# A graph and mixture-of-experts kernel: quads to octets, and routed tiles inside the gather stage from per-expert bins in DRAM

## The reference, cut to what matters

```
x = x + gnn(layernorm(x))           # x: 12500 nodes x 256
x = x + ffn(layernorm(x))

gnn(f):  agg[d] = sum over edges (s -> d) of weight * f[s]    # 212,500 edges, sorted by d
         return agg @ W.T + b
ffn(f):  H = gelu(f @ W1 + b1)                 # 256 -> 1024
         probs = softmax(H @ Wg + bg)          # 8 experts
         e = argmax(probs)                     # per node
         return probs[e] * (H @ Wd[e] + bd[e])  # 1024 -> 256
```

## Time and profile before

| what | before |
|---|---|
| median of 3 runs | 3659.71 us (3659.63 to 3661.93) |
| profiled execution | 3686.61 us, span 3684.6 us |
| granted TensorE clock, mean | 0.706 of full speed |
| busy PE, POOL | 56%, 49% of the span |
| busy DVE, ACT | 31%, 12% |
| moved by DMA | 420.31 MB, mean 114 GB/s |

### The profile page before, as it was taken

How to read it: one execution, slowest core, us unless ns; L and a number is a source line. 1 busy time by engine, 2 the same in 40 slices (tenths; PEclk the granted TensorE clock), 3 DMA queues, 4 the chain that set the end, 5 groups by cost and what they waited for, 6 DMA issues and landing times.

```text
span 3684.6 us, 40719 instructions
## 1 busy us (share of the span) xinstructions
PE 2061.4 (56%) x10526; PEld 1319.5 (36%) x10527; DVE 1151.1 (31%) x3507; ACT 443.2 (12%) x847; POOL 1822.5 (49%) x1988
## 2 busy tenths in 40 slices
PE   0134555455535554455445544555355548599998
PEld 0112332233323332233223322332233324488887
DVE  8121332233323332233223322332133224733332
ACT  5000000000000000000000000000000002043343
POOL 1656445644565445544664455444644540055554
PEclk9995666566656666566656656666566658799999
DMA  8323332333333332333233323332333231455554
GB/s 358 88 82 98 97 103 84 115 99 98 104 91 106 100 101 83 113 100 101 84 115 100 102 81 111 98 102 86 105 103 100 82 92 63 154 180 180 181 184 139
DMA packets 153598, 420.31 MB, mean 114 GB/s; under 512 B 33320, under 2 KB 67499, under 8 KB 150880
## 3 DMA queue, kind: packets, MB, share of 16 engines
q0 software_dynamic: 100032, 300.27, 27.6%
q1 hardware_dynamic: 53536, 119.73, 8.8%
HBM read 328.02 MB, written 92.82 MB: 114 GB/s over the span
## 4 chain that ended last, share of the span: by engine, by line
PE 38%; another core or an unknown queue 33%; issue 15%; DVE 7%; DVEq 5%; ACT 1%; DMA 0%; POOL 0%; ACTq 0%; POOLq 0%
PE psH L557 8%; PE psE L507 6%; PE psA L638 3%; PE psG L638 2%; PE psH L638 2%; PE psE L638 2%; PE psA L578 2%; PE psG L499 2%; PE psR L499 2%; PE psA L535 2%; DVEq L301 2%; DVE rows L942 1%; DVEq L295 1%; PE psG L564 1%
## 5 line engine op out<-in xcount | busy, mean ns | idle before, releaser
L387 POOL DMA_INDIRECT big<-xn_table,src_i x1664 | 1590.8, 956 | 1427.4 <-PE psG L499 620.8
L507 PE MATMUL psE<-place,parts 128*128 128x64 f32 x1664 | 450.8, 433 | 1015.3 <-DVE parts L853 778.4
L507 PEld LDWEIGHTS psE<-place,parts 128*128 128x128 f32 x1664 | 382.6, 324 | 1280.6 <-DVE parts L853 871.7
L557 PE MATMUL psH<-xn2T,w 128*128 128x512 f32 x800 | 427.9, 692 | 128.6 <-issue 64.5
L450 ACT ACTIVATE hidT<-psH,b 128x512 f32<-128x512 f32 x200 | 136.4, 687 | 2447.2 <-remote 1006.6
L499 PE MATMUL psR<-big,sel_narrow 128*32 128x256 f32 x1664 | 216.8, 613 | 289.4 <-issue 289.4
L557 PEld LDWEIGHTS psH<-xn2T,w 128*128 128x128 f32 x800 | 173.4, 223 | 347.8 <-issue 267.6
L860 DVE TENSOR_TENSOR big<-psE,big 128x128 f32 x416 | 121.2, 291 | 545.1 <-remote 294.3
L853 DVE COPY parts<-psR 128x256 f32<-128x256 f32 x208 | 88.0, 423 | 518.6 <-remote 461.2
L499 PE MATMUL psG<-big,sel_narrow 128*32 128x256 f32 x1664 | 217.6, 613 | 0.0
L864 DVE TENSOR_TENSOR place<-iota,shift_f 128x256 f32<-128x256 f32 x104 | 44.4, 427 | 447.7 <-issue 447.7
(11 more groups left out here) (194 smaller groups left out, 2193.4 us busy)
## 6 DMA issues: line engine op xcount, KB each, us to landing
row_table<-rows SPq DMA_DIRECT2D x25, 2064.0 KB
big<-xn_table,src_i POOLq DMA_INDIRECT x1664
big<-in_x SPq DMA_DIRECT2D x10, 1280.0 KB, 17.5
xn_table<-big SPq DMA_DIRECT2D x10, 1280.0 KB, 12.9
big<-in_x SPq DMA_DIRECT2D x25, 512.0 KB
row_table<-big SPq DMA_DIRECT2D x25, 512.0 KB, 3.0
big<-in_Wd SPq DMA_DIRECT2D x8, 1024.0 KB, 12.0
hidT<-in_dstT SPq DMA_DIRECT2D x2, 840.0 KB, 30.3
```

The source lines that it names most:

```text
L387: nc.gpsimd.indirect_dma_start(out=xring[:, h * STEP_TILES + j, :], out_offset=None, in_=xn_dram[:, :], in_offset=bass.IndirectOffsetOnAxi ...
L507: mm = nc.tensor.matmul(psE[q % 2][:, k * NARROW:(k + 1) * NARROW], parts[:, q % 2, k * P:(k + 1) * P], place[:, q, :], start=True, stop=True)
L557: mm = nc.tensor.matmul(psH[c % 2][:, :], w1[:, k, c * P:(c + 1) * P], xn2T[:, k, :], start=(k == 0), stop=(k == KC - 1))
```

## The change

**Octets.** A gather step is now two octets of 8 tiles. All 16 partial matmuls run in a row and raise `s_edge_mm` once, by 16; DVE copies both octets at once (128x512), PE places both (8 matmuls for a window of 80 nodes each in place of 64) and signals once, DVE adds twice. The weights of the next step's one-hots come behind the additions.

**The group step** is split into part A and part B, and with `LATER = 0` a group's part B stands directly behind its part A. Part A is the GNN product, the residual and the normalisation, with two routed tiles on PE beside it. Part B is the transposes, `hidden` and the logits, two more routed tiles, then the sort of the group's own 512 nodes by expert: rank matmuls over one-hots, a permutation as a matrix (DVE), 16 matmuls of 128x260 that put the rows in order, ACT copies, a store to `sorted_dram`, and 15 DRAM-to-DRAM copies of blocks into one bin per expert (`bin_dram`), from places that a plan made by DVE names. Rows in the bins are 260 wide: residual or normalised values and the probability, not the 1024 hidden values, which are neither transposed nor stored any more.

**A routed tile** is 128 rows of one bin. It loads the rows, the 1 MB of its expert's weights and the bias on SP, in a ring of two; it computes hidden anew (16 matmuls of 128x128 and 8 gelus), then multiplies by the expert's weights (8 matmuls), and its result goes to `done_dram`. 4 tiles per group make 100 early tiles (the first groups' have nothing to work on but run), and 16 late tiles follow behind the last group. When all gathers are issued and read, POOL brings back the 100 early results and scatters them, 16 at a time from the three sections, then the late ones. The routing of all nodes at once, and the loading of all weights, are gone.

The accumulator's ring has 6 slots in place of 8, and the PSUM banks are laid out anew. Core of the diff:

```diff
-QUAD = 4
-QUADS = STEP_TILES // QUAD
-NARROW = 64
 SECTIONS = 3
+OCT = 8
+OCTS = STEP_TILES // OCT
+SPAN = 80
 LANES = 32
+HALF_LANES = 16
...
+STEPS = NG + ITEMS
+LATER = 0
...
+            def load_tile(r, row, expert):
+                i = r % RING2
+                if r >= RING2:
+                    sp.wait_ge(s_o2, r - RING2 + 1)
+                sp.dma_start(xr[:, i, :], bin_dram[bass.ds(row, P), :]).then_inc(s_xl[i], 16)
+                sp.dma_start(wd[:, i, :, :].rearrange("p c o -> p (c o)"),
+                             Wd[bass.ds(expert, 1), :, :].rearrange("a p f -> p (a f)")).then_inc(s_wl[i], 16)
...
+            def store_tile(r):
+                sp.wait_ge(s_o2, r + 1)
+                sp.dma_start(done_dram[r * P:(r + 1) * P, :], obuf[:, r % RING2, :]).then_inc(s_os[r % RING2], 16)
...
+                sp.wait_ge(s_plan, f + 2)
+                for a in range(0, BLOCKS, 5):
...
+                    for one, other in zip(froms, tos):
+                        sp.dma_start(bin_dram[bass.ds(other, BLOCK), :],
+                                     sorted_dram[bass.ds(one, BLOCK), :]).then_inc(s_cp, 16)
...
+            for f in range(NF):
+                r0, r1, r2, r3 = tiles_of(f)
+                plan = tile_plan(0, PER_GROUP)
+                sp.sem_inc(s_seen, 1)
+                load_tile(r0, *plan[0])
+                load_tile(r1, *plan[1])
+                store_tile(r0)
+                load_tile(r2, *plan[2])
+                if f < LAST:
+                    sp.wait_ge(s_xn2, f + 1)
+                    load_x(f + 1)
+                store_tile(r1)
+                load_tile(r3, *plan[3])
+                store_tile(r2)
+                store_tile(r3)
+                nq = QB if f < LAST else LAST_QB
+                sp.wait_ge(s_ev, f * QB + nq + 1)
+                sp.dma_start(sorted_dram[0:nq * P, :].rearrange("(q p) c -> p q c", p=P),
+                             sorted_rows[:, 0:nq, :]).then_inc(s_sst, 16)
+                sp.wait_ge(s_sst, 16 * (f + 1))
+                copy_blocks(f)
...
+            def scatter_batch(b):
+                h = b % SECTIONS
+                pool.wait_ge(s_back[h], 16 * (b // SECTIONS + 1))
+                for j, r in enumerate(batches[b]):
+                    scatter(xring[:, h * STEP_TILES + j, :], r, s_out[h])
...
+            for b in range(len(batches)):
+                scatter_batch(b)
+                if b + SECTIONS < len(batches):
+                    bring_back(b + SECTIONS)
+            for j in range(REST):
+                pool.wait_ge(s_o2, EARLY + j + 1)
+                scatter(late_rows[:, j, :], EARLY + j, s_out[0])
...
+            def gelu_routed(r):
+                for c in range(HC):
+                    if c % 4 == 0:
+                        act.wait_ge(s_h2, r * 2 + c // 4 + 1)
...
+                copy_routed(r0)
+                gelu_routed(r0)
+                copy_routed(r1)
+                residual(r0)
+                gelu_routed(r1)
+                residual(r1)
+                hidden(f, nq)
+                copy_routed(r2)
+                gelu_routed(r2)
+                copy_routed(r3)
+                residual(r2)
...
+                gelu_routed(r3)
+                residual(r3)
+                if f > 0:
+                    act.wait_ge(s_sst, 16 * f)
+                for t in range(nq):
+                    act.wait_ge(s_srt, f * QB + t + 1)
+                    nc.scalar.activation(sorted_rows[:, t, :], psH[t % 2][:, 0:ROW], ACT.Identity).then_inc(s_ev, 1)
...
-                        for j in range(QUAD):
-                            t = h * STEP_TILES + q * QUAD + j
-                            mm = nc.tensor.matmul(psQ[q % 2][j * LANES:(j + 1) * LANES, 0:C], sel_narrow[:, t, :],
-                                                  xring[:, t, :], start=True, stop=True)
-                        mm.then_inc(s_edge_mm, QUAD)
                         for k in range(KC):
-                            mm = nc.tensor.matmul(psE[q % 2][:, k * NARROW:(k + 1) * NARROW],
-                                                  parts[:, q % 2, k * P:(k + 1) * P], place[:, q, :],
-                                                  start=True, stop=True)
-                        mm.then_inc(s_placed, 1)
+                    pe.wait_ge(s_narrow, g + 1)
+                    for o in range(OCTS):
+                        for odd in range(2):
+                            for j in range(OCT // 2):
+                                t = h * STEP_TILES + o * OCT + 2 * j + odd
+                                mm = nc.tensor.matmul(psQ[j * LANES:(j + 1) * LANES, o * C:(o + 1) * C],
+                                                      sel_narrow[:, t, :], xring[:, t, :],
+                                                      start=(odd == 0), stop=(odd == 1))
+                    mm.then_inc(s_edge_mm, STEP_TILES)
+                    pe.wait_ge(s_parts, g + 1)
+                    for o in range(OCTS):
                         for k in range(KC):
+                            at = (o * KC + k) * SPAN
+                            mm = nc.tensor.matmul(psE[:, at:at + SPAN], parts[:, o, k * P:(k + 1) * P],
+                                                  place[:, o, :], start=True, stop=True)
+                    mm.then_inc(s_placed, 1)
...
+            def routed_hidden(r, i):
+                pe.wait_ge(s_c2, r + 2)
+                for c in range(HC):
+                    if c % 4 == 0:
+                        pe.wait_ge(s_g2, r * HC + c + 4)
+                    for k in range(KC):
+                        mm = nc.tensor.matmul(psH[c // 4][:, (c % 4) * P:(c % 4 + 1) * P],
+                                              w1[:, k, c * P:(c + 1) * P], xT2[i][:, k * P:(k + 1) * P],
+                                              start=(k == 0), stop=(k == KC - 1))
+                    if c % 4 == 3:
+                        mm.then_inc(s_h2, 1)
...
+                for c in range(HC):
+                    pe.wait_ge(s_g2, r * HC + c + 1 + HC)
+                    mm = nc.tensor.matmul(psY[:, 0:C], hT2[:, c, :], wd[:, i, c, :],
+                                          start=(c == 0), stop=(c == HC - 1))
+                mm.then_inc(s_y2, 1)
+            def routed_pair(r, rounds, between=None, then=None):
+                transposes(r, 0, rounds)
+                if between:
+                    between()
+                routed_hidden(r, 0)
+                if then:
+                    then()
+                transposes(r + 1, 1, rounds)
+                product(r, 0, rounds)
...
+            def part_a(f, nq):
                 pe.wait_ge(s_aggs, f + 1)
+                for q in range(nq):
+                    for k in range(KC):
                         mm = nc.tensor.matmul(psA[q // 2][:, (q % 2) * C:(q % 2 + 1) * C],
                                               aggs[:, k, q * P:(q + 1) * P], wt[:, k, :],
+                                              start=(k == 0), stop=(k == KC - 1))
                 mm.then_inc(s_z, 1)
+                pe.wait_ge(s_ev, f * QB + 1)
+                routed_pair(f * PER_GROUP, f * 2)
+                second_of_pair(f * PER_GROUP + 1, f * 2)
...
+                routed_pair(f * PER_GROUP + 2, f * 2 + 1, gate, lambda: pe.wait_ge(s_dif, f + 1))
+                pe.wait_ge(s_oh, f + 1)
...
+                second_of_pair(f * PER_GROUP + 3, f * 2 + 1)
+                pe.wait_ge(s_perm, f + 1)
+                for t in range(nq):
+                    if t >= 2:
+                        pe.wait_ge(s_ev, f * QB + t)
+                    for q in range(nq):
+                        mm = nc.tensor.matmul(psH[t % 2][:, 0:ROW], perm[:, q, t * P:(t + 1) * P], ext[:, q, :],
+                                              start=(q == 0), stop=(q == nq - 1))
+                    mm.then_inc(s_srt, 1)
...
                 with pe.If(kind == SECTIONS):
+                    part_a(n.with_bounds(min_val=0, max_val=LAST - 1), QB)
                 with pe.If(kind == SECTIONS + 1):
+                    part_b(n.with_bounds(min_val=0, max_val=LAST - 1), QB)
+            part_a(LAST, LAST_QB)
+            part_b(LAST, LAST_QB)
...
                     nc.vector.tensor_tensor(
+                        place[:, :, :], iota[:, 0:SPAN].unsqueeze(1).to_broadcast([P, OCTS, SPAN]),
...
+                    dve.wait_ge(s_edge_mm, g * STEP_TILES + STEP_TILES + MM0)
+                    nc.vector.tensor_copy(parts[:, :, :], psQ[:, :].rearrange("p (o c) -> p o c", c=C)).then_inc(s_parts, 1)
+                    narrow_onehots(g + 1, start)
+                    dve.wait_ge(s_placed, g + 1)
+                    for o in range(OCTS):
+                        accumulate(o)
+                    narrow_weights(g + 1, start)
                     dve.sem_inc(s_sel, STEP_TILES)
...
+                routed_out(f * PER_GROUP, 0, 0, f * 2)
+                routed_out(f * PER_GROUP + 1, 1, 1, f * 2)
...
```

(46 more changed lines are left out.)

1058 lines of the change are left out of this document (513 added, 545 removed).

## The result

The changed kernel takes 4460.34 us (4442.84 to 4483.0, 4 runs) against 3659.67: a ratio of 1.219, 95% interval 1.214 to 1.225. The forecast was 4600, the range 4000 to 4950.

What follows compares the result with a forecast made beforehand. No engine is full in the gather stage; POOL and PE take turns, as PE's signals inside bursts are seen late. 3684.6 + 1265 + 20 − 37 − 302 + 8 = 4639, scaled to about 4600 us; range 4000 to 4950.

Steps and rivals of the forecast that it cites:

- The mechanism: Gather stage: the group step is serial on PE, gather steps keep the pace of POOL's bursts; chance 0.62.
- +1265 + 20 − 37: Gather stage: 23 longer blocks +1265 us, the first group +20, the gather steps −37.
- The block: Group step, from its burst's start to the next: 99 us against 44.1, +55 each, 23 times.
- PE's stretch from the GNN product to the next partials: Group step: rest of A 20.0 us, B 49.0, loops 2.4 each.
- +23.2, as before: Group step: GNN product visible at DVE 23.2 us after the burst's start, unchanged.
- R3: Rival, gather stage: more signals held or code loaded, steps of 28 us or 10 more per block, about 4975; chance 0.10.
- the tail: From the 24th group's start to the end: 351 us in place of 653, −302.
- Gather steps: Between group steps: bursts still 23.1 us apart against 23.6, −37 us in all.
- The loads of the weights: Gather stage: four 1 MB loads per group lie beside PE's work and cost nothing.
- DVE's 0 to +230: Part B: DVE's longer work taken as 0, bounds 0 to 10 us a group.
- R1: Rival, gather steps: signals in time for every second step, period 152 us, whole about 4100; chance 0.13.
- R2: Rival, gather stage: signals on time, POOL's gathers overlap the block, period stays at 120 us, about 3345; chance 0.15.

Runs made afterwards that it cites:

- c_after: The changed kernel itself measured once more, on a chip where PE's signals inside bursts come late (held chip): 4425 us, 1.228 of the kernel before.
- e6: Changed kernel with an eighth of each expert's weights loaded, 128 KB in place of 1 MB per routed tile: 4415 us, ratio 1.225.
- e1_later1: Changed kernel with part B one gather step behind part A, on a chip where PE's signals come on time: 4159 us, ratio 1.475.
- e8h: Kernel before with POOL waiting mid-burst until its first 8 gathers have landed, on a held chip: 3682 us, ratio 1.0003.
- e3h: Changed kernel with POOL waiting mid-burst until its first 8 gathers have landed, on a held chip: 4406 us, ratio 1.199.
- the last run: Changed kernel without the never-taken wide-step branch and with part B one gather step later, on an on-time chip: 2997 us, ratio 1.062.
- e4h_half: Changed kernel with half of every routed tile's matmuls left out, on a held chip: 4265 us, ratio 1.163.

## Why the prediction was right, and where it was off

**The mechanism held.** The group step is one serial block of PE, the gather steps in between go at the pace of POOL's bursts, and the two add: +1032 us over 23 periods. I forecast +1265 + 20 − 37 = +1248. Of the signs, POOL's long waits came as 25 of 67 us on the mean (23 of some 75 forecast), the group starts 165.5 us apart (174), the late tiles 7.25 (8 to 10), and the clock in the gather stage at 0.72 (0.65).

**The block** was forecast at 99 against 44.1. On the mean of the 23 intervals between bursts that hold one it is 93.0 (46.7 on 24 before, by the same count, where I had used one example of 44.1), so it grew by 46 and not by 55; that is most of the 216 us by which the periods came out shorter. The mis-sized term is PE's stretch from the GNN product to the next partials: 73.7 with the loops in the forecast, 61.9 on the mean. 128x128 records cost 0.12 us (3.83 for 32) and not 0.134, the lower clock that I paid 2.0 for was 0.72 on the stage's mean and not 0.62 (0.95 in a whole block of c_after, 1392 to 1462), and the handoffs are shorter, as the second pair's work stands ready. The other error has the opposite sign: the "+23.2, as before" to the product is +28.8 on the mean. More than half of that was there before, since the example of the earlier trace rows was an early one (26.5 on the mean); the change added 2.3, with the placements' signal held in most groups, which is the first half of rival R3. That the sum lay within 4% is in part luck: the tail, below, was too short by 42 in the forecast and took back some of what the block was too long.

**Gather steps:** 22.7 us on the mean of 80, forecast 23.1; by the same count they were 22.8 before, so the octets changed nothing here.

**Costed at nothing.** The loads of the weights were (e6: no change). DVE's 0 to +230 was not nothing, but was not DVE's operations either: it was code. I had loading of code in R3 at up to 10 us a block. DVE's idle is 10.2 us ahead of each gather step (4.3 in the kernel before), some four times a period, and taking the unused code out gives 1.7% on a held chip.

**The tail** is 393, forecast 351. The last group took 4166.4 to 4270 on PE, 104 us for 57 forecast, beside POOL's 100 scatters, for which I had added 40. Then PE waits for the first late tile:

```profile
PE psT L612 <- issue: 57.4, 1, 57.4
```

with SP issuing the 15 block copies behind each other in that time (start, duration):

```profile
4139.25 15.92 SPq L380 DMA_DIRECT2D expert_bins<-sorted_rows  x15
...
4276.93 46.77 SPq L380 DMA_DIRECT2D expert_bins<-sorted_rows  x15
```

The last group's store, copies, plan and first load were forecast at 20 us and took 57, the tail's mis-sized term. The first of the two lines is the group before, in a stretch in which POOL issues nothing: 15.92 us for the same 15 copies, close to what I had priced. Beside POOL's scatters they took 46.77, beside a burst of gathers 28.42 (from 1149.66). Why SP issues slower there is open. The late tiles took 7.25 us each for 8.2.

**The rivals.** R1 (every second step on time) did not come: of 80 intervals between bursts 22 are under 21.2 us, one in four, and not one in two. R2 (overlap comes back) was argued from signals on time. There are chips where signals are on time, so R2's premise is real, but the changed kernel itself never ran on one. The best version of it there gets 1.06, since the kernel before gains still more. My estimate of an octet's step, 9.5 us, is mostly 8.1 in that run (7.0 to 9.9), and R2's period, 120, is 107.

## What to carry to other kernels

Before an engine's wait is priced, look whether the releaser's record and the waiter's start agree: where they differ, the pace is set by something that the listing does not name, and it may be of the chip and not of the kernel. Take the mean over all steps and not one example: the two blocks that I compared, 44.1 and 100.5 us, are an early one and the latest of all, and the means are 46.7 and 93.0. When a change makes the body of a loop with branches longer, compare the packets of the queue for code before anything else; a branch that is never taken cost 28% of one version's time here. A block that is put into an in-order engine's stream costs its whole length less what the ring ahead of it holds, and shortening it pays only down to the next engine's chain; where PE then waits it can lose clock too.

## What the runs showed of the hardware that I had not expected

**Signals inside a burst of indirect gathers are late on some chips and not on others.** In c_after the recorded end of PE's partials falls into a burst in 78 of 104 steps, and by the semaphore's events in the trace their signal comes 5.0 to 15.6 us behind it in 76 of these; in the 26 steps outside of a burst it comes within 0.3 us. In e1_later1, which differs in `LATER` alone, it comes within 0.1 us in all 104 steps, 56 of them inside a burst. The two times of the kernel before, 2821 and 3595 to 3675, go with this. A pause of some 2.5 us in POOL's issues lets part of the signals through (e8h, e3h). What in the chip does it is open, and so is whether a matmul whose signal is held ran on time. The Trainium skill's rule on computed ends (Perfetto Trace Analysis, "Tensor Engine Instruction (MATMUL, LD_WEIGHTS)"), weighed in the prediction, stays untested; the 1 to 3 us more a step that the partials would have cost by it did not come (22.7 us for 22.8).

**Code is loaded at each turn of a loop that has grown too long.** Packets of 8 KB, 815 against 59 with the branch out, spread evenly over the gather stage at some 50 per 250 us (c_after): the 756 more are some 5 for each of the 152 turns of the changed loop. DVE's idle ahead of a gather step was 4.3 us in the kernel before (447.7/104), 10.2 in the changed one, 13.3 with part B a step later, and 2.4 without the branch. So not all of this idle is code: the kernel before has 4.3 with 23 packets. The Trainium skill (Runtime: NRT & Kernel Launch, "Instruction fetch mechanics") says that code is fetched ahead only in sequence, and that a branch to a place outside what is loaded stops the engine until that is fetched. By that rule the kernel with its long loop bodies would show idle without a releaser at each change of branch; the runs agree, with the numbers above.

**TensorE's granted clock rose with the longer block.** 0.62 in the gather stage before (PE busy 52% of it), 0.72 in the changed kernel's (52%), 0.85 on the mean of the last run (75% of the span). The busy share alone does not tell the first two apart. In e4h_half, with shorter work and waits of some 4.7 us inside the block, it fell to 0.68 in the gather stage.
